# Every 56th gather tile of layer 0 and every 72nd of layer 1 moved from GpSimd to SyncE, row by row

## The reference, cut to what matters

```python
h = relu(layernorm(x))
x = x + segment_sum((h @ W0.T + b0)[src] * edge_weight[:, None], dst)          # layer 0
h = relu(layernorm(x))
for t in range(4):                                                            # layer 1
    m = relu(concat(h[src], h[dst]) @ W1[t] + b1[t]) @ W2[t] + b2[t]
    msgs += where(edge_type == t, m, 0)
agg = segment_sum(msgs, dst)
r, z, n = gates(agg @ W_ih.T + b_ih, h @ W_hh.T + b_hh)
x = x + (1 - z) * n + z * h
```

## Time and profile before

| | |
|---|---|
| median of 3 runs | 2152.25 us (2151.32 to 2152.91) |
| the profiled execution | 2151.11 us |
| its span, first to last instruction | 2149.4 us |
| GpSimd busy | 1585.1 us (74%) |
| TensorE busy | 1275.7 us (59%) |
| VectorE busy | 900.7 us (42%) |
| ScalarE busy | 569.6 us (27%) |
| share of the chain that ended last: GpSimd, issue | 73%, 24% |
| mean granted TensorE clock, share of 2.4 GHz | 0.743 |

### The profile page before, as it was taken

How to read it: one execution, slowest core, us unless ns; L and a number is a source line. 1 busy time by engine, 2 the same in 40 slices (tenths; PEclk the granted TensorE clock), 3 DMA queues, 4 the chain that set the end, 5 groups by cost and what they waited for, 6 DMA issues and landing times.

```text
span 2149.4 us, 23739 instructions
## 1 busy us (share of the span) xinstructions
PE 1275.7 (59%) x6652; PEld 1084.8 (50%) x6652; DVE 900.7 (42%) x2535; ACT 569.6 (27%) x1502; POOL 1585.1 (74%) x1677
## 2 busy tenths in 40 slices
PE   2445445445455455454556677677777776776775
PEld 2434334334344343343346666666666666666665
DVE  7732233233233233233234555545545545545554
ACT  4623333333333323333231111111111111111111
POOL 6777777777777777777567777777777777777774
PEclk7566666566666666566677987888888798888888
DMA  8323223223233223223244444444444444444442
GB/s 181 94 79 98 78 79 99 77 79 99 77 80 99 77 79 98 77 79 99 59 127 112 105 115 110 112 111 112 113 112 109 113 116 106 114 116 108 115 112 54
DMA packets 176204, 213.84 MB, mean 99 GB/s; under 512 B 53644, under 2 KB 121962, under 8 KB 175569
## 3 DMA queue, kind: packets, MB, share of 16 engines
q0 software_dynamic: 53248, 109.16, 21.2%
q1 hardware_dynamic: 121577, 102.33, 16.4%
q10 hardware_dynamic: 1244, 0.79, 0.2%
HBM read 176.56 MB, written 35.56 MB: 99 GB/s over the span
## 4 chain that ended last, share of the span: by engine, by line
POOL 73%; issue 24%; PE 1%; DMA 1%; DVE 1%; ACT 0%; POOLq 0%; SPq 0%; DVEq 0%; ACTq 0%
POOL accs L1248 36%; POOL G L1581 15%; POOL edge L1581 15%; POOL g_more L1581 7%; DMA accs<-in_edge_weight_dram 0%; PE bank L1522 0%; DMA accs<-h_tab,src_t 0%; PE bank L1485 0%; DMA edge<-p_tab,src_t 0%; DMA p_tab<-hot 0%; PE bank L1785 0%; PE bank L1762 0%; ACT accs L1402 0%; PE bank L1775 0%; PE bank L1786 0%
## 5 line engine op out<-in xcount | busy, mean ns | idle before, releaser
L1248 POOL DMA_INDIRECT accs<-h_tab,src_t x776 | 732.7, 944 | 236.5 <-issue 236.2
L1752 PE MATMUL bank<-qwin,hotT 128*128 128x128 f32 x1664 | 292.4, 330 | 313.8 <-DVE hotT L1646 302.6
L1485 PE MATMUL bank<-accs 128*125 128x133 f32 x1664 | 334.4, 372 | 227.1 <-ACT accs L1402 177.1
L1485 PEld LDWEIGHTS bank<-accs 128*125 128x125 f32 x1664 | 312.0, 274 | 270.8 <-issue 132.2
L1752 PEld LDWEIGHTS bank<-qwin,hotT 128*128 128x128 f32 x1664 | 246.8, 228 | 352.7 <-DVE hotT L1646 340.6
L1581 POOL DMA_INDIRECT G<-p_tab,src_t x336 | 320.0, 952 | 126.3 <-issue 103.0
L1581 POOL DMA_INDIRECT edge<-p_tab,src_t x336 | 318.9, 949 | 102.4 <-issue 102.4
L1402 ACT ACTIVATE accs<-accs,edge 128x128 f32<-128x128 f32 x776 | 247.6, 391 | 492.7 <-DMA accs<-h_tab,src_t 491.9
L1710 ACT ACTIVATE rows<-rows 128x512 f32<-128x512 f32 x208 | 130.9, 629 | 673.2 <-DVE rows L1654 673.2
L1762 PE MATMUL bank<-hot,rows 128*128 128x128 f32 x1664 | 285.9, 329 | 5.8 <-ACT rows L1710 5.2
L1762 PEld LDWEIGHTS bank<-hot,rows 128*128 128x128 f32 x1664 | 268.9, 245 | 6.2 <-ACT rows L1710 6.2
(11 more groups left out here) (175 smaller groups left out, 1332.0 us busy)
## 6 DMA issues: line engine op xcount, KB each, us to landing
qwin<-q_tab SPq DMA_DIRECT2D x416, 64.0 KB
nodew<-key_tab SPq DMA_DIRECT2D x52, 256.0 KB
nodehot<-key_tab SPq DMA_DIRECT2D x52, 256.0 KB, 3.6
accs<-h_tab,src_t POOLq DMA_INDIRECT x776, 2.6
p_tab<-st SPq DMA_DIRECT2D x25, 224.0 KB
p_tab<-hot SPq DMA_DIRECT2D x25, 224.0 KB
q_tab<-st SPq DMA_DIRECT2D x25, 224.0 KB
q_tab<-hot SPq DMA_DIRECT2D x25, 224.0 KB
```

The source lines that it names most:

```text
L1248: eng.indirect_dma_start(slot0(o % R0)[:, t, 0:D], None, x if o < EARLY else h0_tab, bass.IndirectOffsetOnAxis(src_t[:, k:k + 1], 0)).then ...
L1485: ins = eng.matmul(pb[SUM_BANK[o % 4]][0:CW, 0:FW], ones_of(o % HR)[:, t, :], slot0(o % R0)[:, t, :], start=t == 0, stop=t == TO - 1)
L1752: ins = eng.matmul(pb[2 + g % 2][:, t * D:(t + 1) * D], hotT[:, g % HT, t * P:(t + 1) * P], qwin[:, g % NG, t // PR, :], start=True, stop= ...
```

## The change

SyncE fetches 13 whole tiles of layer 0 (the last tile of octets 15, 22, ..., 99) and 11 of layer 1 (the last tile of groups 22, 40, ..., 202), each with 128 DMAs of one row, and in both layers the ten rows of tile 830. The row numbers come from HBM (`src` in layer 0, the new `row_tab` in layer 1) into one partition of SBUF, and are read into SyncE's registers up to eight at a time. The 128 rows of a tile are issued over seven octets or over 18 groups, ahead of their use; two tile buffers (`row_alone0`, `row_alone1`) alternate. GpSimd leaves these tiles out and also the empty tile 831, as do ScalarE and TensorE. ScalarE reads the tile from its own buffer (`weigh`), VectorE adds it in a second instruction (`total`). SyncE's loop over pairs in layer 0 is turned into a loop over octets, in which the stores of p and of q of a pair stand in their own octets and rows between them. In the prologue ScalarE converts the row numbers of layer 1 to integers and SyncE stores them.

```diff
+        ALONE0 = [((6 + 7 * j + 9) * TO + TO - 1, [(6 + 7 * j + i, P * i // 7, P * (i + 1) // 7) for i in range(7)]) for j in range(13)]
+        ALONE0.append((NTILE - 1, [(97, 0, E - (NTILE - 1) * P)]))
+        ALONE1 = [((2 + 18 * j + 20) * GT + GT - 1, [(2 + 18 * j + i, P * i // 18, P * (i + 1) // 18) for i in range(18)]) for j in range(11)]
+        ALONE1.append((NTILE - 1, [(202, 0, E - (NTILE - 1) * P)]))
+        rows_no0 = hotT[0:1, 0, P:3 * P].bitcast(I32)
+        rows_no1 = w1b[0:1, 0:2, :].rearrange("p a d -> p (a d)").bitcast(I32)
...
+        def sp_row_numbers(eng):
+            eng.wait_ge(s["row_no"], 1)
+            eng.dma_start(row_tab.rearrange("(p e) -> p e", p=PB), typ_i.rearrange("p g e -> p (g e)")).then_inc(s["row_st"], 16)
+        def row_values(eng, numbers, a, b, top):
+            _, v = nc.values_load_multi_w_load_instructions(
+                numbers[0:1, a:b], engines=[eng.engine], min_val=0, max_val=top,
...
+        def act_row_numbers(eng):
+            eng.wait_ge(s["keys_in"], 1)
+            eng.activation(typ_i, src4_a, ACT.Copy).then_inc(s["row_no"], 1)
...
         def f0_pool(eng):
...
                     k = o * TO + t
+                    if k in alone0 or k >= NTILE:
+                        continue
...
             def weigh(o):
...
+                        if k in alone0:
+                            j = alone0[k]
+                            eng.wait_ge(s_a0[j % 2], rows_alone(ALONE0, j))
+                            row = row_alone0(j)
+                        ins = eng.activation(G0[:, t, 0:D], row, ACT.Copy, scale=w_t[:, o * TO + t:o * TO + t + 1])
...
         def f0_sp(eng):
...
+            def rows_by_number(j, a, b):
+                if a == 0:
+                    numbers(j + 1)
+                    eng.wait_ge(s_no0[j % 2], 16 * (j // 2 + 1))
+                    if j >= 2:
+                        eng.wait_ge(s["dv0"], 2 * (ALONE0[j - 2][0] // TO) + 2)
+                for i in range(a, b, 8):
+                    n = min(8, b - i)
+                    v = row_values(eng, rows_no0, j % 2 * P + i, j % 2 * P + i + n, N - 1)
+                    for r in range(n):
+                        eng.dma_start(row_alone0(j)[i + r:i + r + 1, :], h0_tab[bass.ds(v[r], 1), :]).then_inc(s_a0[j % 2], 16)
+            numbers(0)
+            eng.wait_ge(s["tab"], 32 * len(T_PIECES))
+            for o in range(STEPS0 + 1):
+                if (p := pair_at(o, 1)) is not None:
+                    p_rows_out(p)
+                if (p := pair_at(o, 2)) is not None:
+                    q_rows_out(p)
+                if o in issue0:
+                    rows_by_number(*issue0[o])
...
         def f1_sp(eng):
...
+            def rows_by_number(j, a, b):
+                if a == 0:
+                    numbers(j + 1)
+                    eng.wait_ge(s_no1[j % 2], 16 * (j // 2 + 1))
+                    if j >= 2:
+                        eng.wait_ge(s["sum1"], ALONE1[j - 2][0] // GT + 1)
+                for r, v in enumerate(row_values(eng, rows_no1, j % 2 * P + a, j % 2 * P + b, N * T - 1)):
+                    eng.dma_start(row_alone1(j)[a + r:a + r + 1, :], p_rows[bass.ds(v, 1), :]).then_inc(s_a1[j % 2], 16)
...
             for g in range(-2, STEPS1):
...
+                if g in issue1:
+                    rows_by_number(*issue1[g])
...
             def total(g):
...
+                n = next((t for t in range(GT) if g * GT + t in alone1), GT)
+                ins = eng.tensor_tensor(rows[:, g % 2, 0:n], got[:, 0:n], slot1(g % R1)[:, 0:n], ALU.add)
+                if n < GT:
+                    j = alone1[g * GT + n]
+                    eng.wait_ge(s_a1[j % 2], rows_alone(ALONE1, j))
+                    ins = eng.tensor_tensor(rows[:, g % 2, n], got[:, n], row_alone1(j), ALU.add)
```

More of the change, by code:

```diff
@@ L207, in gnn_program, with row_alone0, row_alone1, rows_alone @@
         EARLY = 7
+        ALONE0 = [((6 + 7 * j + 9) * TO + TO - 1, [(6 + 7 * j + i, P * i // 7, P * (i + 1) // 7) for i in range(7)]) for j in range(13)]
+        ALONE0.append((NTILE - 1, [(97, 0, E - (NTILE - 1) * P)]))
+        ALONE1 = [((2 + 18 * j + 20) * GT + GT - 1, [(2 + 18 * j + i, P * i // 18, P * (i + 1) // 18) for i in range(18)]) for j in range(11)]
+        ALONE1.append((NTILE - 1, [(202, 0, E - (NTILE - 1) * P)]))
+        alone0, alone1 = ({k: j for j, (k, _) in enumerate(a)} for a in (ALONE0, ALONE1))
+        issue0, issue1 = ({o: (j, a, b) for j, (_, part_s) in enumerate(al) for o, a, b in part_s} for al in (ALONE0, ALONE1))
+        assert NTILE == NT - 1 and NTILE % GT == 3
+        def row_alone0(j):
+            return hotT[:, 2, j % 2 * D:(j % 2 + 1) * D]
+        def row_alone1(j):
+            return w1a[:, j % 2, :]
+        rows_no0 = hotT[0:1, 0, P:3 * P].bitcast(I32)
+        rows_no1 = w1b[0:1, 0:2, :].rearrange("p a d -> p (a d)").bitcast(I32)
+        def rows_alone(al, j):
+            return 16 * sum(b - a for _, part_s in al[j % 2:j + 1:2] for _, a, b in part_s)
+        def gathered0(o, h):
+            return 16 * sum(o_ * TO + t not in alone0 and o_ * TO + t < NTILE
+                            for o_ in range(o % R0, o + 1, R0) for t in range(h * GT, (h + 1) * GT))
+        def gathered1(g):
+            return 16 * sum(g_ * GT + t not in alone1 and g_ * GT + t < NTILE for g_ in range(g % R1, g + 1, R1) for t in range(GT))
         key16 = accs[0:PB, K16:K16 + ECOL // 2].bitcast(BF16)
@@ L269, in gnn_program @@
         s_xl = [sem(f"s_xrows{q}") for q in range(2)]
+        s_a0 = [sem(f"s_alone0_{q}") for q in range(2)]
+        s_a1 = [sem(f"s_alone1_{q}") for q in range(2)]
+        s_no0 = [sem(f"s_number0_{q}") for q in range(2)]
+        s_no1 = [sem(f"s_number1_{q}") for q in range(2)]
         s_k = [sem(f"s_keys{q}") for q in range(2)]
@@ L368, in sp_keys @@
             eng.dma_start(key_tab.rearrange("(p e) -> p e", p=PB), key16).then_inc(s["key_st"], 16)
+        def sp_row_numbers(eng):
[4 more added lines that the diff above has]
+                numbers[0:1, a:b], engines=[eng.engine], min_val=0, max_val=top,
+                skip_runtime_bounds_check_because="they are row numbers of the graph's edges, as the gathers read them")
+            return v
         def sp_x(eng):
@@ L1399, in weigh @@
                 for h in range(2):
[L1400 removed]
+                    eng.wait_ge(s_g0[o % R0][h], gathered0(o, h))
                     for t in range(h * GT, (h + 1) * GT):
[L1402 removed]
+                        k, row = o * TO + t, G0[:, t, 0:D]
+                        if k >= NTILE:
+                            continue
+                        if k in alone0:
[3 more added lines that the diff above has]
+                        ins = eng.activation(G0[:, t, 0:D], row, ACT.Copy, scale=w_t[:, o * TO + t:o * TO + t + 1])
                     ins.then_inc(s["dv0"], 1)
@@ L1481, in octet @@
                     eng.wait_ge(s["acc0"], o - 3)
-                for t in range(TO):
+                last = min(TO, NTILE - o * TO) - 1
+                for t in range(last + 1):
                     if t % GT == 0:
@@ L1485, in octet @@
                     ins = eng.matmul(pb[SUM_BANK[o % 4]][0:CW, 0:FW], ones_of(o % HR)[:, t, :], slot0(o % R0)[:, t, :],
-                                     start=t == 0, stop=t == TO - 1)
+                                     start=t == 0, stop=t == last)
                 ins.then_inc(s["out0"], 1)
@@ L1551, in f0_sp, with p_rows_out @@
                     eng.dma_start(h0_lin[h, a:b, :], t_rows[i][h]).then_inc(s["tab"], 16)
-            for p in range(NPAIR):
+            def p_rows_out(p):
                 if p + 2 < NPAIR:
@@ L1750, in expand @@
                     eng.wait_ge(s["sum1"], g - 1)
-                for t in range(GT):
+                for t in range(min(GT, NTILE - g * GT)):
                     ins = eng.matmul(pb[2 + g % 2][:, t * D:(t + 1) * D], hotT[:, g % HT, t * P:(t + 1) * P],
@@ L1759, in sums @@
                     eng.wait_ge(s["acc1"], (g - 1) * GP)
-                for t in range(GT):
+                last = min(GT, NTILE - g * GT) - 1
+                for t in range(last + 1):
                     p = t // PR
                     ins = eng.matmul(pb[4 + g % 2][:, p * KEYS:(p + 1) * KEYS], rows[:, g % 2, t, :], hot[:, g % NG, t, :],
-                                     start=t % PR == 0, stop=t % PR == PR - 1)
+                                     start=t % PR == 0, stop=t % PR == PR - 1 or t == last)
                 ins.then_inc(s["out1"], 1)
```

32 lines of the change are left out of this document (25 added, 7 removed).

## The result

The changed kernel takes 2706.81 us (median of 4, 2703.3 to 2709.55) against 2152.58 us (2151.32 to 2154.84): ratio 1.2572, 95% interval 1.2551 to 1.2594. It is slower, as forecast, but by 554 us instead of 132, and far outside the range of 2112 to 2440. The profiled execution has a span of 2701.5 us.

The account below looks back on a forecast made before the run. GpSimd bounds the kernel before; SyncE was to become the bound in both layers. Span = 692 + 1609 x 0.529 + 1408 x 0.525 = 2282, plus 1.7, gives 2284 us, range 2112 to 2440.

Parts of the forecast that it names:

- The rooms of 0.475 and 0.437 us per row: SyncE's time for each new row within GpSimd's pace: 0.475 us in layer 0, 0.437 in layer 1.
- The waits: GpSimd was to wait on out0 late in layer 0 and on sum1 through most of layer 1.
- At nothing: Prologue table, VectorE's split addition (uncovered under 10 us) and moved p and q stores (delayed at most 10 us): no cost.
- Small DMAs are not dearer: Denies a rival: one-row DMAs on SyncE cost 0.355 us, a row 0.63, formula 2580 us; chance of dearer 0.09.
- Reading the numbers into registers: SyncE's loads of row numbers into registers: 0.084 us per row in layer 0, 0.080 in layer 1.
- my upper bound of 0.63: Highest cost of one row on SyncE, in us; taken were 0.529 in layer 0 and 0.525 in layer 1.
- the formula: Above c = 0.50, span = 692 + 1609 c(layer 0) + 1408 c(layer 1), in us; it gave 2282.
- c: SyncE's cost per one-row DMA with register work and number loads: 0.529 us in layer 0, 0.525 in layer 1.
- the likeliest case: SyncE is the bound with c from 0.49 to 0.59: 2175 to 2450 us, chance 0.64.
- the rows fit: Rival: at c of at most 0.437 us SyncE keeps GpSimd's pace, 34.9 us come off, 2117 us; chance 0.18.

Follow-up runs that it names:

- j3: Changed kernel with row numbers read into registers once a layer, all 3092 row DMAs kept, wrong rows fetched: 2111.68 us against 2154.69 for the kernel before, ratio 0.9806.
- h1: Changed kernel with the pieces of row numbers cut at multiples of eight: 2339.73 us against 2149.82 for the kernel before, ratio 1.0883.
- e1: Changed kernel with the pieces of row numbers cut at multiples of eight, measured where the kernel before takes 2550 to 2552 us: 3208.78 us, ratio 1.2582.
- e2: The kernel of e1 with every load of row numbers starting one place further: 3497.42 us, one run, against 3208.78 for e1.
- e6: Changed kernel with fewer tiles on SyncE, cut at multiples of eight, layer 1's rows right behind window loads: 2118.02 us against 2150.39 for the kernel before, ratio 0.9847.
- The aligned kernel: Changed kernel with the pieces of row numbers cut at multiples of eight, the kernel of e1 and h1: 3208.78 us in e1, 2339.73 us in h1.
- g3: The same edit as j3, measured where the kernel before takes 2550 to 2552 us: 2726.16 us, ratio 1.0679.

## Why the prediction was wrong

**Right.** GpSimd was the bound and SyncE became it, in both layers. The rooms of 0.475 and 0.437 us per row are bracketed, not measured: j3's rows cost 0.32 and fit, h1's cost 0.54 and don't. The forecast of slower was not luck: h1, whose loads cost 0.11 and 0.10 us per row, close to the 0.08 that I took, is still 8.8% slower, and its 2339.73 us lie in the range. The waits came where they were named, on `out0` and on `sum1` through most of layer 1, but those on `out0` begin at 380 us and not late, the groups come every 6.5 us and not 5.5, and layer 1 begins at 1334 and not 1120. "At nothing" holds as well: in j3 the table's store, VectorE's split addition and the moved p and q stores are all there, and it is 43 us faster. Small DMAs are not dearer: 228 ns, inside the bounds of 0.22 to 0.355 and below the 0.255 taken; the address work ahead of one is 37 ns where the window's was 46, so that a row without its loads costs 0.427 and 0.432 us with gaps, 0.445 predicted. I had read the rule of the Trainium skill on missing increments (DMA: Bandwidth & Descriptors, Why a DMA increments its semaphore by 16 and not by 1) as a sign of a dear small DMA. The issue time doesn't bear that reading out: a row of one partition takes 228 ns, a window of 128 takes 357. Who writes the increments, no run here shows.

**The step that failed** is "Reading the numbers into registers", the term (0.63 + 0.63 + 0.27) / 18.3 = 0.084 us per row in layer 0 and 0.080 in layer 1. It measured 0.236 and 0.225 with its gaps. SyncE's cost per row came to 0.663 and 0.657 us, beyond my upper bound of 0.63, which only a dearer DMA was to reach. I took SyncE's 307 ns for four values and added VectorE's 64 ns for each further one. Both rows are of loads that start at a multiple of four; what a load costs from another place was in no row, and I neither asked nor gave this term bounds of its own, although reached to 914 and 1358 ns. 1358 per load would have been 0.19 us per row in layer 1, 0.22 in layer 0, and with it the formula gives about 2660. The floor of 600 ns that the Trainium skill gives (DMA: Bandwidth & Descriptors, Latency and other measured facts) is no floor here, since loads of bases took 293 and loads of row numbers 532 ns at the least. An estimate with the page's figure gives 0.11 and 0.09 us per row, half of what came or less; the page says nothing of the place.

The formula itself stands, with one slip: at c = 0.59 it gives 2474 and not the 2450 that I set as the likeliest case's upper end. With the measured c it gives 692 + 1609 x 0.663 + 1408 x 0.657 = 2684 us for a span of 2701.5, where the prediction had 2282. Of the difference of 420 us the loads make 1609 x 0.152 + 1408 x 0.145 = +449, the cheaper DMAs 1609 x 0.018 + 1408 x 0.013 = -47, and 17 are left. Layer 0 comes out at 1336 us for its end by the formula, 1334.4 measured. SyncE's own work in layer 1, which I had at 1.82 us a group, took more than those 17: it has 1335 us for 206 iterations (line 823, 1339.3 to 2674.4), less 1418 x 0.657, that is 1.96 each and 28 us in 198 groups; the terms for the two ends of the layer were together some 10 us too high. The load of four bases, 307 ns before, takes 562 ns behind rows, and a window DMA 357 where it took 342.

**Shown and not shown.** That the place of the first value makes the loads dear is shown by e1 against e2, and that the dear loads make the difference to 2340 us by h1 against the changed kernel. Why the place matters is not shown. Nor is it why the same load from a multiple of four takes 0.53 us behind windows, 0.78 behind rows and about 1.27 behind stores of h or of output rows (medians of h1); the stores were not moved alone. Of the rivals, "the rows fit" needed rows of at most 0.437 us: j3's cost 0.32, and it came within 6 us of that rival's 2117.

## What to carry to other kernels

Before work moves to a queue that rests, price the whole loop there and not only the instruction it is about: here the DMA cost 0.23 us, about as expected, and filling the registers for it as much again. Give a range of its own to every term whose row has another shape, alignment or neighbour than the new instruction, even if it looks small; each 50 ns per row are 150 us here. And when values are read into registers, try blocks of eight that start at a multiple of four, and compare places in the queue: here they were cheapest right behind the window loads.

## What the runs showed of the hardware

- A load of eight values of 4 bytes into SyncE's registers takes 0.79 us from a multiple of four and 1.93 us from any other place, with the same one-row DMA ahead; seven values 0.95 and 1.48 us behind window loads; two values 0.73 us from either.
- What was issued ahead counts too: from a multiple of four, eight values take 0.53 us behind window loads (e6) and 0.79 behind a one-row DMA; from another place 1.93 behind a row, 2.1 to 3.1 behind a store of h. The load of four bases went from 0.31 to 0.56 us in the median once row DMAs stood in the queue.
- One kernel takes different times: the kernel before took 2150 us in some measurements and 2550 to 2583 in others, and one chip gave both. No trace shows the kernel before at the upper level. In the others' traces there the gathers still take 0.94 us each, but SyncE's one-row DMAs of layer 0 start 0.78 us apart in the mean (e1), 0.42 in h1, the same kernel, though the median is 0.41 in both, and its small instructions have long ones among them. The same group of g3, for which j3 had 29/29/38:

```profile
L1646 SPq MOVE hotT<-h_tab x1674: 1/29/1396, 119.6 to 1355.8; - x186
```

  The aligned kernel's ratio is 1.258 there instead of 1.088. That instructions reach SyncE late would fit a register move of 1.4 us, but no run tests it. What brings the upper level is open.
